# Moving the transposes of the second-layer integer weights from self-attention to the end of cross-attention, and one row load ahead of two bias loads

## The reference

```
x = layernorm(x + self_attention(x))            # pre-norm, causal, one head of 512, residual inside
x = layernorm(x + cross_attention(x, ctx))      # 375 context rows, 16 heads of 32, masked, normed delta
x = layernorm(x + ffn(x))                       # 512 -> 2048 -> 512, gelu

def _quant_per_tensor(x):  scale = max(max|x| / 127, 1e-8);          q = clip(round(x / scale))
def _quant_per_channel(w): scale = max(max|w| over axis 1 / 127, ..); q = clip(round(w / scale[:, None]))
def _dyn_quant_linear(x, w, b):
    return (qx @ qw.T) * (sx * sw) + b
h = _dyn_quant_linear(x, w1, b1);  h = gelu(h);  y = _dyn_quant_linear(h, w2, b2)
```

## Time and profile before

| | |
|---|---|
| median of the runs | 1490.15 us (1488.83 to 1490.62) |
| profiled execution, its own time | 1488.81 us |
| its span, first to last instruction | 1487.0 us |
| mean granted clock of TensorE | 0.991 of full speed |
| PE, DVE, ACT, POOL busy | 97%, 71%, 44%, 39% of the span |
| DMA | 93 GB/s over the span |

### The profile page before, as it was taken

How to read it: one execution, slowest core, us unless ns; L and a number is a source line. 1 busy time by engine, 2 the same in 40 slices (tenths; PEclk the granted TensorE clock), 3 DMA queues, 4 the chain that set the end, 5 groups by cost and what they waited for, 6 DMA issues and landing times. The chain is left out here.

```text
span 1487.0 us, 33650 instructions
## 1 busy us (share of the span) xinstructions
PE 1440.3 (97%) x13322; PEld 1123.5 (76%) x13322; DVE 1055.3 (71%) x2021; ACT 656.9 (44%) x865; POOL 579.2 (39%) x510
## 2 busy tenths in 40 slices
PE   7899999999899999999999999999999996899898
PEld 3688888887788888888888888888888885455343
DVE  2866565564477777877777778777787777677898
ACT  1333333333343343433433433334333332789996
POOL 0000000000144544555445545454545453753576
PEclk9999999999999999999999999999999998899999
DMA  6023333321511212112111121121111210439895
GB/s 219 29 79 103 103 103 102 102 76 52 184 41 42 73 45 72 39 45 72 45 47 64 45 72 39 45 72 45 56 55 45 72 46 24 107 113 327 274 348 200
DMA packets 80743, 138.59 MB, mean 93 GB/s; under 512 B 5218, under 2 KB 52834, under 8 KB 78898
## 3 DMA queue, kind: packets, MB, share of 16 engines
q1 hardware_dynamic: 80690, 137.87, 28.4%
HBM read 93.82 MB, written 44.04 MB: 93 GB/s over the span
## 5 line engine op out<-in xcount | busy, mean ns | idle before, releaser
L737 POOL TENSOR_TENSOR xa_psum<-xa_pr 125x448 f32<-125x448 f32 x126 | 153.9, 1221 | 236.3 <-DVE xa_pr L883 236.3
L883 DVE TENSOR_SCALAR xa_pr<-xa_pr,xa_keep 125x448 f32<-125x448 f32 x384 | 151.0, 450 | 108.3 <-ACT xa_pr L783 107.0
L783 ACT ACTIVATE xa_pr<-xa_bSC 125x1344 f32<-125x1344 f32 x128 | 165.6, 1293 | 138.3 <-PE xa_bSC L989 132.3
L764 ACT ACTIVATE xa_kf<-xa_bKV,xa_bk 128x376 f32<-128x376 f32 x128 | 73.6, 575 | 184.9 <-PE xa_bKV L913 184.9
L740 POOL TENSOR_TENSOR xa_psum<-xa_psum,xa_pr 125x448 f32<-125x448 f32 x126 | 147.0, 1167 | 12.1 <-POOL xa_psum L737 4.4
L913 PE MATMUL xa_bKV<-left_xn,wA 128*128 128x376 f32 x768 | 149.9, 344 | 0.0
L913 PE MATMUL xa_bKV<-xa_cx,wA 128*128 128x376 f32 x768 | 149.3, 343 | 0.0
L770 ACT COPY xa_v<-xa_bKV 125x512 f32<-125x512 f32 x96 | 56.2, 585 | 206.2 <-PE xa_bKV L924 201.1
L924 PE MATMUL xa_bKV<-wZ,left_xn 128*125 128x512 f32 x576 | 141.9, 394 | 1.7 <-POOL xa_ones L713 1.7
L924 PE MATMUL xa_bKV<-wZ,xa_cx 128*125 128x512 f32 x576 | 141.1, 393 | 0.0
L913 PEld LDWEIGHTS xa_bKV<-left_xn,wA 128*128 128x128 f32 x768 | 130.0, 188 | 8.9 <-issue 5.3
(11 more groups left out here) (193 smaller groups left out, 2508.8 us busy)
## 6 DMA issues: line engine op xcount, KB each, us to landing
wraw<-in_ctxT SPq DMA_DIRECT2D x32, 752.0 KB, 4.8
ff_hr<-h_scratch SPq DMA_DIRECT2D x28, 512.0 KB, 6.5
wraw<-in_w SPq DMA_DIRECT2D x8, 1024.0 KB, 7.7
sa_raw<-in_x SPq DMA_DIRECT2D x8, 896.0 KB, 5.9
x_scratch<-left_qraw SPq DMA_DIRECT2D x8, 896.0 KB, 5.1
xa_qf<-q_scratch SPq DMA_DIRECT2D x32, 224.0 KB, 4.9
xa_x<-x_scratch SPq DMA_DIRECT2D x32, 224.0 KB, 4.7
x_scratch<-xa_x SPq DMA_DIRECT2D x32, 224.0 KB, 2.3
```

The source lines that it names most:

```text
L737: nc.gpsimd.tensor_tensor(psum01[:], third(h, 0), third(h, 1), ALU.add).then_inc(p01_ok, 1)
L783: nc.scalar.activation(pr[h][:], bSC[0:TW, :, 0:TC * S], ACT.Exp, scale=XSCALE).then_inc(exp_ok, 1)
L883: nc.vector.tensor_scalar(third(h, t), third(h, t), EM50, bound, ALU.max, ALU.min).then_inc(pr_ok, 1)
```

## The change

Two edits.

1. The four quarters of w2 are no longer transposed in self-attention. DVE writes their integers untransposed straight into w2q, in 16 blocks of 128 columns with a stride, instead of into `wint`. PE and ACT do nothing for w2 in odd groups, and PE's wait for `u_ok` ahead of L581 is left for even groups alone. At the end of cross-attention PE transposes all 64 blocks of w2q, eight at a time, into the four banks of `bSC`, and ACT copies each eight (1024 columns) back into the place that they came from. POOL builds an identity matrix for it at that part's start.
2. At the start of feed-forward, SP issues the load of group 1's tokens first, then b1, then b2. ACT waits for b1 alone, and b2 has a semaphore of its own, for which POOL waits before layer 2's first use of it.

```diff
             def unit(g, par, pair, f):                       # ACT
-                act.wait_ge(u_turn, 4 * g + f + 1)
                 if par == 0:
+                    act.wait_ge(u_turn, 4 * pair + f + 1)
                     nc.scalar.copy(w1q[:, f, span(pair * D, D)], bW[:, 0:D]).then_inc(u_ok, 1)
-                else:
-                    nc.scalar.copy(w2q[:, C * f:C * f + C, span(pair * P, P)],
-                                   bW[:, 0:D].rearrange("p (m o) -> p m o", m=C)).then_inc(u_ok, 1)
...
                 dve.wait_ge(u_round, 4 * g + 4)              # DVE
-                wait(dve, u_turn, 4 * g)
-                nc.vector.tensor_scalar(wint[:], flat, -ROUND, None, ALU.add).then_inc(u_int, 1)
+                if par == 0:
+                    wait(dve, u_turn, 4 * pair)
+                    nc.vector.tensor_scalar(wint[:], flat, -ROUND, None, ALU.add).then_inc(u_int, 1)
+                else:
+                    nc.vector.tensor_scalar(w2q[:, :, span(pair * P, P)], flat.rearrange("p (m i) -> p m i", m=M), -ROUND, None,
+                                            ALU.add).then_inc(u_int, 1)
...
-            def unit(g, par, f):                             # PE
+            def unit(g, par, pair, f):
+                if par == 1:
+                    return
                 pe.wait_ge(u_int, g + 1)
...
                 pe.wait_ge(pr_ok, 4 * g + 4)
-                pe.wait_ge(u_ok, 4 * g + 4)
+                if par == 0:
+                    pe.wait_ge(u_ok, 4 * pair + 4)
...
+        M2 = M // 2                                          # cross-attention
+        w2_blocks = [(i, w2q[:, i % 2 * M2:(i % 2 + 1) * M2, i // 2 * P:(i // 2 + 1) * P], bSC[:, i % NJ, :].bitcast(BF16)) for i in range(2 * C)]
...
+            nc.gpsimd.memset(identb[:], 0.0).then_inc(const_ok, 1)
+            pool.wait_ge(const_ok, 3)
+            nc.gpsimd.affine_select(out=identb[:], in_=identb[:], compare_op=ALU.not_equal, fill=1.0, base=0,
+                                    pattern=[[-1, P]], channel_multiplier=1).then_inc(const_ok, 1)
...
             steps(act, body, B, 2)
+            for i, ints, bank in w2_blocks:
+                act.wait_ge(w2_turn, i + 1)
+                nc.scalar.copy(ints, bank.rearrange("p (m o) -> p m o", m=M2)).then_inc(w2_ok, 1)
...
             output(B - 1, range(2, C))
+            pe.wait_ge(const_ok, 4)
+            pe.wait_ge(exp_ok, C * B)
+            for i, ints, bank in w2_blocks:
+                wait(pe, w2_ok, i - NJ + 1)
+                for m in range(M2):
+                    mm = nc.tensor.transpose(bank[:, m * P:(m + 1) * P], ints[:, m, :], identb[:])
+                mm.then_inc(w2_turn, 1)
...
-            for t, s in ((b1t, b1), (b2t, row(b2, P))):      # feed-forward, SP
-                sp.dma_start(t[:], s).then_inc(small_in, 16)
-            for g in range(1, RES + 2):
+            load_x(1, 1)
+            sp.dma_start(b1t[:], b1).then_inc(small_in, 16)
+            sp.dma_start(b2t[:], row(b2, P)).then_inc(b2_in, 16)
+            for g in range(2, RES + 2):
                 load_x(g, g % 2)
...
+            pool.wait_ge(b2_in, 16)
             biased(0)
...
-            act.wait_ge(small_in, 32)
+            act.wait_ge(small_in, 16)
```

## The result

The changed kernel takes 1481.69 us in the median of 4 runs (1480.54 to 1486.19), the kernel before 1490.38 us beside it (4 runs, 1488.83 to 1491.41). The ratio is 0.9951, with a 95% interval of 0.9931 to 0.9971. The forecast was 1483.0 us with a range of 1480.8 to 1486.4. Another 6 runs of the changed kernel, in the first experiment, gave 1482.0. One execution among all the runs of this document, of e9_three_filled, ran at a granted clock of 0.654 throughout and took 2041.55 us; the figures of that kernel are given without it.

A forecast was written before the change was run, and what follows sets the result against it. PE was taken to bound self-attention and layer 1, but SP's last store the end of cross-attention. The terms 4.6 + 0.7 + 0 + 1.8 gave 7.1 us off 1490.15, thus 1483.0 us, range 1480.8 to 1486.4.

The forecast's parts named there:

- Term 1: Self-attention: w2 transposes leave PE's odd groups, fifteen sets saving 3.3 us and group 7's last set 1.3, together 4.6 us.
- Term 3: End of cross-attention: the 64 moved transposes and eight copies fit under the layer norm chain and SP's last store, costing 0.
- Term 4: Start of feed-forward: group 1's tokens land sooner, so PE's 1.8 us wait for POOL in layer 1 goes.
- Term 2: Group 7's output product: with one PE pause the clock may stay at 2.4 GHz, gaining 1.4 us or nothing; 0.7 counted.
- The rival that PE gains nothing in the odd groups: Self-attention: a wait that the transposes covered takes their place, giving 1488.3 us; chance 4%.
- The rival in which the tail sticks out: End of cross-attention: ACT's copies end past SP's last store, giving 1484.7 us, or 1487.4 without overlap; chance 8%.
- the slower one: End of cross-attention: PE and ACT take turns at 3 us per eight blocks, giving 1497.8 us; chance 4%.
- The rival of the late b1: Layer 1: b1 lands behind the tokens so late that ACT's gelus are 3.4 us late, giving 1486.4 us; chance 6%.

The follow-up runs named there:

- e9_three_filled: The changed kernel plus filler transposes of the identity in three self-attention pauses of PE (first token transposes, group 0's output, group 7's output): 1478.0 us, ratio 0.9925.
- e1_again: The changed kernel run once more without alteration: 1482.0 us, ratio 0.9947 against the kernel before; its profiled execution takes 1481.17 us.
- e6_copies_twice: The changed kernel with each of the eight ACT copies at the end of cross-attention done twice: 1488.31 us, ratio 0.9986 against the kernel before.
- e3_loads_only: The kernel before plus edit 2 alone (new load order), with self-attention and cross-attention as before: 1485.55 us, ratio 0.9974.
- e4_group7_late: The kernel before with group 7's fourth set of four transposes and its copy moved behind the output product, no work removed: 1488.5 us, ratio 0.9985.
- e5: The changed kernel without the 64 transposes and eight copies at the end of cross-attention, w2 left untransposed: 1483.7 us, ratio 0.9957 against the kernel before.
- e12: The changed kernel with b1 issued ahead of group 1's tokens and b2 behind them: 1481.86 us, ratio 0.9942 against the kernel before.
- e2: The kernel before plus edit 1 alone (w2 transposes moved), with the old order of loads: 1485.03 us, ratio 0.9964.
- e10: Edit 1 alone with the old load order, plus 32 filler transposes in layer 1's pause ahead of group 1's transposes: 1482.54 us, ratio 0.9948 against the kernel before.
- e11: The kernel before, neither edit, with filler transposes in the pauses of self-attention and of layer 1: 1487.94 us, ratio 0.999.
- e8: The changed kernel with fillers in four PE pauses, three in self-attention and one in cross-attention: 1481.39 us, ratio 0.9946 against the kernel before.

## Why the prediction was right

The sum was 7.1 us; 7.3 came out by the ratio, 8.7 by the medians, and 7.6 in e1_again. The terms 1 and 3 are shown. That the sum came out so well is in part luck: term 4 was too small by about 2.2 us, term 2 is not shown to have given the median anything, and edit 1 alone gave 4.5 us (3.1 to 7.6 by the interval) where terms 1 and 2 count 5.3.

**Term 1 (4.6 us) held.** From output to output of groups 1 and 3 it is 197.75 - 113.79 = 83.96 us before and 198.72 - 115.62 = 83.10 after, 0.86 less for four sets; 0.88 was counted. From group 6's output to group 7's it is 32.61 before and 30.57 after: 2.04 less, where 3 x 0.22 + 1.34 = 2.0 was counted. Over groups 1 to 7 that is 0.88 (groups 0 to 1, in e6_copies_twice, whose clock did not fall there) + 1.75 + 2.04 = 4.7 us. The rival that PE gains nothing in the odd groups is out. The row's 48 to 60 ns for a transpose, and not the 81 ns of the Trainium skill (TensorE: Matmul & The Clock Gate, section Back-to-back issue gap), sized it rightly: 0.86 us over sixteen is 54 ns. At 81 ns the pair of groups would be 1.3 us shorter. One detail missed: the output of group 7 was to take under 4 us and takes 4.06.

**Term 2 (0.7 counted, 1.4 if in full) is neither shown nor refuted.** In none of the eight profiles of kernels with one unfilled pause there does the clock fall at 357 us. But of the two with both pauses it falls in before and not in e3_loads_only. One fall is too little to say that one pause prevents it, and counting half against the median was a guess that no run checks. e4_group7_late, which removes a pause, moved the median by 1.05 us, what term 1 alone gives; its interval leaves room for more. What the forecast did not see is that the same happens at two more pauses, at 36 and 73 us, in some executions with either version of self-attention.

**Term 3 (nothing) is shown.** A copy of 1024 columns takes 1.01 to 1.02 us, 0.91 from start to start, as the line between two rows gave it. The end, 10.65 us, is the same with the tail, without it (e5), and gives way when the copies are doubled (e6). The rival in which the tail sticks out is out, and with it the slower one. The clock is at 1.00 from 1254 to 1258 with the transposes and at 0.65 without them (e5), so PE never had to do them at the 1.2 GHz that the forecast allowed for; and it is at 0.50 again when feed-forward starts, as it said.

**Term 4 (1.8 us) was mis-sized; the mechanism was right.** The pause goes and the tokens land in time, as forecast, at 1269.9 in the range of 1268.7 to 1270.5. That b2 was the queue ahead is shown by e12; the share of the last store, which landed 2.3 us after its issue, was not tested. The rival of the late b1 is out: b1 lands at 1270.2, ahead of the 1272.3 from which it would have cost something. But the step took one execution's pause as its whole price. Alone, edit 2 gives 4.0 us (e3), and the profiles show two reasons.

The first is the length of the pause. In the three unfilled profiles with the old order it is 1.81, 2.28 (e4) and 2.88 us (e2). POOL is ready at nearly the same distance from the table load in each, and PE's transposes start 18.0 to 18.5 us behind it; with edit 2 they start 15.3 to 16.3 us behind it. PE waits longer where its clock came back sooner: in before the clock has a mean of 0.55 from 1270 to 1272, 7 to 9 us behind the table load, and in e2 one of 0.65 from 1262 to 1264, 6 to 8 us behind.

The second is the clock behind the pause. From the start of these transposes to the row product it is 93.3 us in seven of the eight profiles with edit 2 and 93.7 in the eighth (e6) and in before, but 94.9 in e4 and 96.2 in e2, where the clock falls. With the pause filled it is 93.3 (e10, e11). Both together: the mean of layer 1 is 113.1 us over the three unfilled profiles with the old order and 109.1 over the eight with the new one, 4.0 less.

Three profiles are few, but the other runs point the same way. Of the 25 runs of before beside e1 to e4, the 13 with a mean granted clock of 0.990 or more take 1486.11 to 1489.55 us, and the 12 below take 1490.8 to 1494.17. With edit 2 alone one run of 12 is below 0.990. Where the clock fell in these runs is not on record. The profile of before, from which the term was taken, was an execution without this fall.

**What was not counted, on the other side.** Edits 1 and 2 alone give 4.5 and 4.0 us and both together 7.6, which is within what the intervals leave open. But in some profiles cross-attention is longer than the 894.4 us of e1_again, and by an amount that goes with one load: the first 752 KB of context. Where it lands 4.8 to 5.5 us after its issue (e1, e2, e9, e12), cross-attention takes 894.37 to 894.40 us. With 6.3 us (e11) it is 895.28, with 6.7 (e10) 895.44, with 7.4 (e6) 895.94, with 7.9 (e5) 896.36 and with 7.7 (after) 897.79. In before, e3 and e4 it lands after 4.9 to 5.2 us. The place, in the timeline of after:

```profile
393.24 1.45 ACT L768 CAST xa_cx<-wraw 128x1504 fp32r<-128x1504 f32 x1 [2.21 <-DMA wraw<-in_ctxT]
...
398.72 2.95 DVE L896 TENSOR_SCALAR xa_pr<-xa_pr,xa_keep 125x448 f32<-125x448 f32 x3
...
403.07 1.46 POOL L750 TENSOR_TENSOR xa_psum<-xa_psum,xa_pr 125x448 f32<-125x448 f32 x1
...
404.58 0.56 PE L988 MATMUL xa_bPV<-xa_psum,xa_ones 125*32 125x112 f32 x8 [1.92 <-POOL xa_psum L750]
405.07 3.69 PE L926 MATMUL xa_bKV<-left_xn,wA 128*128 128x376 f32 x12
```

and in e1_again:

```profile
397.12 1.18 DVE L896 TENSOR_SCALAR xa_pr<-xa_pr,xa_keep 125x448 f32<-125x448 f32 x3 [2.08 <-ACT xa_pr L793]
...
401.24 0.40 PE L988 MATMUL xa_bPV<-xa_psum,xa_ones 125*32 125x112 f32 x8 [0.17 <-POOL xa_psum L750]
401.56 2.35 PE L926 MATMUL xa_bKV<-left_xn,wA 128*128 128x376 f32 x12
```

In after the load lands 2.2 us too late for ACT, ACT's first two exponentials of the part start 2.79 us apart instead of 4.97, DVE's second masking takes 2.95 us instead of 1.18 (it now runs beside POOL's first sum, and one of its three steps takes 1.34 us), POOL's sums are late, PE waits 1.92 us, and behind the wait the clock is down (0.61 from 404 to 407), so that twelve products take 3.69 us instead of 2.35. In e5 PE waits 1.91 us at the same place and the clock stays at 1.00 behind it, which makes up most of the 1.4 us between the two. The order of events can be read off the trace. Why the load is late is open; e11 is the kernel before with fillers, so edit 1 is not needed for it, and whether the change makes it more frequent these profiles are too few to say. No experiment changed it by itself.

## What to carry to other kernels

Price a pause of TensorE twice: once by its length and once by what runs at 1.2 GHz behind it, and look for both in more than one profiled execution, since the length varies (1.81 to 2.88 us here) and the fall comes and goes. Work for an idle engine behind the last use of a bank is free only up to the engine that is late anyway; measure the room (here 1.3 us left) and not the share. In one queue, put what the bound engine's chain needs ahead of wide loads that nobody needs yet, and check that the small load behind it is not asked for sooner.

## What the runs showed that was not expected

- Pauses of PE of 1.9 to 2.9 us end with the clock at 1.2 GHz in some executions and not in others, with the same instructions around them, and the length does not decide it. The pause ahead of the first token transposes was 2.54 us in both e1 and e5, and the clock fell only in e5; group 0's pause of 1.89 us was followed by the output at full speed in before (four matmuls in 1.97 us) and with the clock down in after (eight in 5.42 us, against 3.9 to 4.0 in the groups behind).
- 32 transposes of an identity in such a pause keep the clock at 1.00 and cost the data's path nothing; three such fillers take the changed kernel to 1478.0 us, against 1481.86 of e12 on the same chip, though the intervals still overlap. Where the pause does not come, they cost their 2.0 us (e8).
- An 8 KB load right behind one of 896 KB in the same queue took 7.0 us instead of 1.9.
- SP's issue of the queries' load in cross-attention (L686, xa_qf) takes 1.08 to 1.33 us in the seven profiles that have edit 1 and no fillers in self-attention and 1.22 in e11, and 0.43 in before, e3, e4, e8 and e9. The context's load is issued right behind it. It lands late (6.3 us or more) in five of the eight profiles with the long issue and in none of the five with 0.43; the cause is open. e9 is one of the five, so a part of its lead over the changed kernel may be this and not the clock.
